# VectorE adds the token biases of more quads: half quads in block 1, four late quads of block 0

## What is computed

```
h   = tanh(ctx@Ws [:, None, t, :] + norm(x)@W [:, f, None, :] + b)     # (2, 2048, 77, 512)
rho = einsum('bftd,d->bft', h, w) + mask                               # scores
att = softmax(rho, over the 77 tokens)
x   = x + tanh(att@ctx@Wcw + bcw) * norm(x) + tanh(att@ctx@Wcb + bcb)
g   = silu(fp4(norm(x)) @ fp4(w_gate).T) * (fp4(norm(x)) @ fp4(w_up).T)
out = x + fp4(g) @ fp4(w_down).T
```

## Time and profile before

| | |
|---|---|
| median of 3 runs | 1538.8 us (1537.33 to 1539.91) |
| profiled execution | 1539.24 us, span 1537.4 us |
| busy: PE, ACT, DVE, POOL | 93%, 88%, 75%, 16% of the span |
| mean granted PE clock | 0.989 of full |
| block 0 scored | until about 352 us |
| quads 7 to 76 of block 1 scored | 385 to 671 us |
| tanhs: plain, 128 x 1024 | 1156 ns mean, 4 to a quad |
| tanhs: summed, 128 x 4096 | 3640 ns mean |
| sum on VectorE, 128 x 1024 | 750 ns mean, 4 to a quad |

### The profile page before, as it was taken

The page is one execution under the profiler, slowest core; times in us unless marked ns, Lnnn a source line. Parts: engine busy times, 40 slices in busy tenths (PEclk is TensorE's granted clock), DMA queues, the critical chain, the costliest instruction groups (busy, mean ns, idle before and its releaser), DMA issues.

```text
span 1537.4 us, 24122 instructions
## 1 busy us (share of the span) xinstructions
PE 1432.1 (93%) x9752; PEld 647.7 (42%) x9752; DVE 1157.2 (75%) x1783; ACT 1359.6 (88%) x1249; POOL 248.7 (16%) x389
## 2 busy tenths in 40 slices
PE   7988889856999999999999999989999999999998
PEld 4444444411333333334444444434444444555564
DVE  4699997944586666759666776698877787898887
ACT  5999989999999999999999999999999999433321
POOL 0122222200111010111011111011101111312211
PEclk9999999988999999999999999999999999999999
DMA  5133332320011111201111111112111111123332
GB/s 159 42 83 83 83 82 75 95 65 8 8 26 41 40 27 41 40 15 40 41 40 40 41 33 37 36 40 40 40 41 41 40 41 40 40 59 73 80 69 62
DMA packets 181557, 77.91 MB, mean 51 GB/s; under 512 B 163627, under 2 KB 165675, under 8 KB 181445
## 3 DMA queue, kind: packets, MB, share of 16 engines
q1 hardware_dynamic: 180224, 75.00, 21.0%
q10 hardware_dynamic: 1221, 1.36, 0.3%
HBM read 27.85 MB, written 8.39 MB: 24 GB/s over the span
## 4 chain that ended last, share of the span: by engine, by line
PE 52%; ACT 27%; DVE 17%; issue 2%; DMA 1%; POOL 1%; SPq 0%; ACTq 0%; DVEq 0%; POOLq 0%
PE rho L809 19%; ACT hring L628 17%; PE dn L906 10%; PE gu1g L892 5%; PE gu0g L892 5%; PE gu1u L892 5%; PE gu0u L892 5%; ACT hring L623 4%; DVE featT L985 2%; ACT wd_room L628 2%; DVE work L1019 2%; ACT featT L623 1%; ACT featT L628 1%; DVE work L1040 1%; DVE work L1039 1%
## 5 line engine op out<-in xcount | busy, mean ns | idle before, releaser
L628 ACT ACTIVATE hring<-featT,bias 128x1024 f32<-128x1024 f32 x688 | 729.2, 1156 | 2.6 <-PE rho L809 2.5
L809 PE MATMUL rho<-hring,wslide 128*32 128x512 f32 x3776 | 459.0, 611 | 61.5 <-ACT hring L628 52.4
L809 PEld LDWEIGHTS rho<-hring,wslide 128*32 128x32 f32 x3776 | 105.5, 111 | 338.6 <-issue 191.7
L628 ACT ACTIVATE featT<-featT,bias 128x1024 f32<-128x1024 f32 x220 | 236.3, 1178 | 2.2 <-PE rho L809 2.2
L906 PE MATMUL dn<-wd_room,turned 128*128 128x512 f16 x1023 | 230.6, 380 | 0.2 <-DMA turned<-work 0.2
L490 POOL TENSOR_SCALAR split_t<-sm 128x32 f32<-128x32 f32 (+4 forms) x82 | 19.7, 240 | 1178.1 <-DVE sm L1008 1178.1
L623 ACT ACTIVATE hring<-featT 128x4096 f32<-128x4096 f32 x57 | 207.5, 3640 | 0.4 <-DVE featT L985 0.4
L985 DVE TENSOR_SCALAR featT<-featT,bias 128x1024 f32<-128x1024 f32 x256 | 175.5, 750 | 11.9 <-ACT hring L623 7.6
L1309 DVE TENSOR_TENSOR work<-sg,gu1u 128x352 f32<-128x352 f32 x64 | 33.3, 521 | 173.9 <-ACT sg L661 173.1
L906 PEld LDWEIGHTS dn<-wd_room,turned 128*128 128x128 f16 x1023 | 96.4, 98 | 145.2 <-issue 36.0
L809 PE MATMUL rho<-featT,wslide 128*32 128x512 f32 x1056 | 126.4, 596 | 5.4 <-ACT featT L628 3.1
(11 more groups left out here) (228 smaller groups left out, 1578.5 us busy)
## 6 DMA issues: line engine op xcount, KB each, us to landing
xt<-in_x SPq DMA_DIRECT2D x32, 256.0 KB, 2.8
out<-xt SPq DMA_DIRECT2D x32, 256.0 KB, 2.3
work<-in_x SPq DMA_DIRECT2D x8, 512.0 KB, 4.1
xt<-in_x SPq DMA_DIRECT2D x6, 512.0 KB, 4.3
xt<-in_L_ffn_w_gate SPq DMA_DIRECT2D x11, 256.0 KB, 2.7
xt<-in_L_ffn_w_up SPq DMA_DIRECT2D x11, 256.0 KB, 3.0
work<-in_L_ffn_w_down SPq DMA_DIRECT2D x2, 704.0 KB, 5.1
xt<-in_L_ffn_w_down SPq DMA_DIRECT2D x2, 704.0 KB, 4.1
```

Source lines behind the costliest of these rows:

```text
L628: act.activation(slot[s][:, g, :], featT[:, e, ROW0[k]:ROW0[k] + rows], ACT.Tanh, bias=bias[:, e, base + tok:base + tok + 1]).then_inc(tan ...
L809: last = pe.matmul(rho[SLOTW * g:SLOTW * g + SLOTW, hf * 512:hf * 512 + 512], wslide[:, e, SLOTW - 1 - r:2 * SLOTW - 1 - r], slot[s][:, g, ...
```

## The change

Three sets of sums are added; nothing else is computed differently.

1. `LATE_SUMS`: the last four quads of block 0 (73 to 76). Quads 73 and 75 go to a room made of two pieces, `stage` and the first 2048 columns of `turned`; ACT takes two tanhs over 2048 columns. Quads 74 and 76 go to `work`, one tanh each. The sum of 73 stands behind the last `down_weights`, the other three behind the wait for `wd_turned`, all ahead of `softmax_drain(0)`.
2. Whole quads 6 and 8 of block 1, and with them the half quads 7 and 9: a new call of `sum_quads` behind `rows_tile(0)` makes these four.
3. Half quads 7, 9, 13, 16, 19, ... 73 of block 1 (23 of them): VectorE adds the biases of the first two parts into `stage` (two instructions), ACT takes one tanh over 2048 columns and two biased ones. The room `stage` is single, so a half waits until ACT has read the half before. Each half stands in VectorE's list where `sum_quads` comes to its number: 13 behind `rows_tile(1)`, 16 behind sum 15, 19 behind product 1 of tile 1 (ahead of `rows_tile(2)`), 22 behind product 2, 25 in the middle of `quantise_hidden(1)`, and so on.

The counts of `summed` are now kept in parts of a quad, because a half adds two. The lists of blocks 2 and 3 keep their quads and rooms.

```
+    LATE_SUMS = (73, 74, 75, 76)
...
+    ROOM_STAGE, ROOM_TURNED, ROOM_WORK = 4, 5, 6
...
+    for m, room in zip(LATE_SUMS, (ROOM_TURNED, ROOM_WORK, ROOM_TURNED, ROOM_WORK)):
+        give_room(m, room)
+    WHOLE = {1: [6, 8, *range(12, QPB, 3)], 2: [3, *range(11, QPB, 4)], 3: [2, 5, *range(11, QPB, 3)]}
+    HALF = {1: [7, 9, *range(13, QPB - 3, 3)], 2: [], 3: []}
     for k in range(1, NBLK):
...
+        for q in sorted([*WHOLE[k], *HALF[k]]):
+            if q in HALF[k]:
+                give_room(QPB * k + q, ROOM_STAGE)
+            else:
+                give_room(QPB * k + q, 0 if k == 1 else 1 + WHOLE[k].index(q) % (k - 1))
...
+        pieces = [[featT[:, :, ROW0[i]:ROW0[i] + 1024]] for i in range(NBLK - 1)] + [[slot[3]]]
+        pieces += [[rows_of(stage[:, :])], [rows_of(stage[:, :]), rows_of(turned[:, 0:2048])], [rows_of(work[:, 0:4096])]]
...
                 if n in SUMMED:
-                    act.wait_ge(summed, GRP * (SUMMED[n] + 1))
-                    act.activation(slot[s], rooms[room_of[n]], ACT.Tanh).then_inc(tanh_ready, GRP)
-                    return
+                    act.wait_ge(summed, SUMMED[n])
+                    at = 0
+                    for piece in pieces[room_of[n]]:
+                        count = piece.shape[1]
+                        act.activation(slot[s][:, at:at + count, :], piece, ACT.Tanh).then_inc(tanh_ready, count)
+                        at += count
+                    part = range(at, GRP)
...
-                for g in range(GRP):
+                rows = [piece[:, i, :] for piece in pieces[room_of[n]] for i in range(piece.shape[1])]
+                for g, row in enumerate(rows):
...
             down_weights(3)
+            sum_quad()
             dve.wait_ge(wd_turned, 16 * KC)
+            for _ in LATE_SUMS[1:]:
+                sum_quad()
...
             rows_tile(0)
+            sum_quads(before[0, 0] - 2)
```

More of the change, by code:

```diff
@@ L111, in bass_xattn_fp4_ffn, with give_room @@
     assert n == QUADS
[L112 to L116, removed]
-    for k in range(1, NBLK):
[L118 to L123, removed]
+    ROOM_STAGE, ROOM_TURNED, ROOM_WORK = 4, 5, 6
+    last_in = {r: QPB * (r + 1) - 1 for r in range(NBLK - 1)}
+    last_in.update({NBLK - 1: None, ROOM_STAGE: None, ROOM_TURNED: None, ROOM_WORK: None})
+    summed_quads, room_of, room_from = [], {}, {}
+    def give_room(m, room):
+        room_of[m], room_from[m] = room, last_in[room]
+        last_in[room] = m
+        summed_quads.append(m)
+    for m in FIRST_SUMS:
+        give_room(m, NBLK - 1)
+    for m, room in zip(LATE_SUMS, (ROOM_TURNED, ROOM_WORK, ROOM_TURNED, ROOM_WORK)):
+        give_room(m, room)
+    WHOLE = {1: [6, 8, *range(12, QPB, 3)], 2: [3, *range(11, QPB, 4)], 3: [2, 5, *range(11, QPB, 3)]}
+    HALF = {1: [7, 9, *range(13, QPB - 3, 3)], 2: [], 3: []}
+    for k in range(1, NBLK):
+        for q in sorted([*WHOLE[k], *HALF[k]]):
[3 more added lines that the diff above has]
+                give_room(QPB * k + q, 0 if k == 1 else 1 + WHOLE[k].index(q) % (k - 1))
     LAST = NBLK - 1
     FREE_FROM = BASE[LAST] - 2
-    SUMMED = {m: i for i, m in enumerate(summed_quads)}
+    rows_summed = [2 if room_of[m] == ROOM_STAGE else GRP for m in summed_quads]
+    SUMMED = {m: sum(rows_summed[:i + 1]) for i, m in enumerate(summed_quads)}
     SOFTMAX_AT = {BASE[k] - 2: k for k in range(1, NBLK)}
@@ L215, in bass_xattn_fp4_ffn, with rows_of @@
                 wd_room[:, 0:4096].rearrange("p (g c) -> p g c", g=GRP), featT[:, :, ROW0[-1]:]]
-        rooms = [featT[:, :, ROW0[i]:ROW0[i] + 1024] for i in range(NBLK - 1)] + [slot[3]]
+        def rows_of(area):
+            return area.rearrange("p (g c) -> p g c", c=1024)
+        pieces = [[featT[:, :, ROW0[i]:ROW0[i] + 1024]] for i in range(NBLK - 1)] + [[slot[3]]]
+        pieces += [[rows_of(stage[:, :])], [rows_of(stage[:, :]), rows_of(turned[:, 0:2048])], [rows_of(work[:, 0:4096])]]
         xnT2 = [stage[:, i * 1024:i * 1024 + 1024].rearrange("p (k r) -> p k r", k=KC) for i in range(2)]
@@ L981, in sum_quad @@
                     dve.wait_ge(tanh_ready, GRP * (room_from[n] + 1))
-                for g in range(GRP):
+                rows = [piece[:, i, :] for piece in pieces[room_of[n]] for i in range(piece.shape[1])]
+                for g, row in enumerate(rows):
                     r, e = quad_at(q) if q < QPB - 1 else (FULLR, g)
                     tok = BATCH_OF[k] * TOK + GRP * r + (g if q < QPB - 1 else 0)
-                    dve.tensor_scalar(rooms[room_of[n]][:, g, :], featT[:, e, ROW0[k]:ROW0[k] + BLOCKS[k]],
+                    dve.tensor_scalar(row, featT[:, e, ROW0[k]:ROW0[k] + BLOCKS[k]],
                                       bias[:, e, tok:tok + 1], None, ALU.add).then_inc(summed, 1)
```

## The result

The changed kernel took 1541.8 us in the median of 14 runs (1540.28 to 1543.44), the kernel before 1538.91 us in runs on the same chips. The ratio is 1.002, its 95% interval [1.0012, 1.0029]: some 3 us slower, where the forecast was 0.7 us slower and the range 1533.5 to 1542.5. The execution profiled took 1542.41 us with a span of 1540.6, that is 3.2 us more span than before.

The account below looks back on a forecast made before the run. ACT bounds block 1 as long as VectorE delivers its sums in time. +1.0 us after two tiles and -0.3 for the rest make +0.7 on 1538.8: 1539.5 us, range 1533.5 to 1542.5.

Parts of the forecast that it names:

- the last score: End of block 1: its last score was to come within 2 us of 670.9.
- Unit prices: On ACT a whole sum saves 0.65 us, a half quad 0.22; on VectorE a half sum costs 1.35 us.
- the straight line: Half tanh on ACT: 1.86 us, between 1.04 for 1024 columns (biased) and 3.51 for 4096 (unbiased).
- Part 1: Last four quads of block 0: all sums in time, block 0 ends 2.2 us earlier.
- Part 2: Quads 6 to 9 of block 1: ACT waits 2.4 us at quad 6, against 1.3 + 0.44 us saved.
- (d): Rival, end of block 0: slow PE clock makes the late sums worth 1.7 us less, 1541; with (c) beyond the forecast 0.07.
- Part 3: Tiles 0 and 1 of block 1: halves 16 and 19 add 2.7 us on VectorE; quad 21 at 442.0, 1.0 us later.
- Part 4: Block 1 from quad 22: 18 halves save 4.0 us, waits cost 4.35, old waits of 0.7 go: net -0.3 us.
- 0.5 us for PE: Block 1 from quad 22: ACT's waits for PE, counted within the 4.35 us of waits.
- The sum: End of block 1: +1.0 - 0.3 = +0.7 us on 1538.8, giving 1539.5.
- (a): Rival, block 1: VectorE hides the sums and all 8.5 us arrive, 1530.3; partly hidden 1533 to 1535; chance 0.22.
- (b): Rival, tiles 2 to 6: VectorE falls behind in each, 2.6 + 1.3 us against 0.8 saved, 1555; chance 0.08.
- (c): Rival, block 1: a half saves 0 (1543) or 0.33 us (1538); with (d) beyond the forecast 0.07.

Follow-up runs that it names:

- more early sums: Changed kernel without whole 6 and halves 16, 19, 49, 61, but with quad 9 summed whole and quad 10 half: 1533.9 us, 0.997 of the kernel before.
- the price alone: Changed kernel, but VectorE adds the 23 halves and ACT makes those quads with four biased tanhs: 1542.16 us, 1.002 of the kernel before.
- the spared version: Changed kernel without whole quad 6 and the halves of 16, 19, 49 and 61: 1533.55 us, 0.9965 of the kernel before.

## Why the prediction was right, and which term was mis-sized

The mechanism was right: VectorE was nowhere near full, and still gave the savings back by coming late at six places, and ACT's wait at each has the length forecast to within 0.15 us. At the mark the change costs 2.3 us where 0.7 were forecast, inside the range. That it was no more is in part luck: ACT's waits, less those of before, came to 12.4 us against the 9.3 forecast (4.6 + 1.0 + 4.35 - 0.7), and the savings were 1.6 us larger too. One of its signs failed: the last score was to end within 2 us of 670.9 and ended at 673.49. By its steps:

**Unit prices.** A half tanh takes 1.80 us start to start, not 1.86, so a half quad saves 0.28 and not 0.22. The estimate from the Trainium skill (ScalarE: Activation LUTs, What ACT_TABLE_LOAD costs), 1.80 because the unbiased tanh has no bias pointer to pay for, was the better price; the straight line mixed two kinds of tanh. The end that the prediction drew from it, 1538.7, is the further off, since the missing waits weigh more. All savings together: 2.4 + 1.3 + 23 x 0.28 = 10.1 us, 1.6 more than forecast.

**Part 1.** Right; block 1's first tanh came 2.3 us earlier (2.2 forecast), and the late quads alone are 0.9991.

**Part 2.** Right in the wait of 2.4 us, incomplete in what follows it. PE idles for 4.05 us while ACT waits, and its score of quad 6 is then slow:

```profile
379.80 3.42 PE L829 MATMUL rho<-hring,wslide 128*32 128x512 f32 x16 [4.05 <-ACT hring L642]
```

3.42 us instead of 1.92. The granted clock of PE over 376 to 384 us was 0.79 of full here and 1.00 in the kernel before (first this kernel, then the one before):

```profile
376.00:384.00 8.00, 4.20 (x22) 1.19 (x23) 4.42 (x8) 7.87 (x5) 0.00 (x0) 0.79 0.01 2
```

```profile
376.00:384.00 8.00, 5.68 (x45) 2.12 (x46) 0.00 (x0) 8.00 (x9) 0.00 (x0) 1.00 0.16 30
```

Those 1.5 us come back to ACT as the wait of 1.16 us at quad 10: ACT may be only two quads ahead of PE, and PE, late with quad 6 and without a gap from there on, scores quad 8 behind two gate groups. The kernel before had its slow stretch too, one that cost it nothing: over 370 to 376 us its granted clock was 0.54 and its score at 371.93, of quad 4, took 3.64 us. In all five kernels in which ACT waits at quad 6 PE is idle for 4.04 to 4.08 us there and scores it in 3.39 to 3.64 us. Of the seven without that wait five score it in 1.92 or 1.93 us. The other two, the one with more early sums (2.87 us after 2.24 of idle time) and the one without the sums of quads 6 to 9, have a slow score too:

```profile
377.08 3.01 PE L829 MATMUL rho<-hring,wslide 128*32 128x512 f32 x16 [2.23 <-ACT hring L648]
380.02 2.53 PE L912 MATMUL gu0g<-wgu,turned 128*128 128x352 f16 x12
```

There ACT, with longer quads behind it, waits only 0.19 us at quad 10. So the slow clock costs something where ACT is at the end of its two slots. The prediction had the clock as a rival, (d), but at the end of block 0; it struck at quad 6 and again ahead of quad 65.

**Part 3.** The path on VectorE was right: 29.4 + 2.7 us. Its start was 1.1 us later than forecast, 0.8 by the wait at quad 10 (less what was saved beyond the forecast) and 0.25 because this execution was that much later already at 308 us, and so was its end: quad 21 at 443.03 and not 442.0. On VectorE:

```profile
430.70 0.52 DVE L1333 TENSOR_TENSOR work<-sg,gu0u 128x352 f32<-128x352 f32 x1
431.25 0.52 DVE L1333 TENSOR_TENSOR work<-sg,gu1u 128x352 f32<-128x352 f32 x1
431.81 1.42 DVE L1006 TENSOR_SCALAR stage<-featT,bias 128x1024 f32<-128x1024 f32 x2
...
440.18 2.74 DVE L1006 TENSOR_SCALAR featT<-featT,bias 128x1024 f32<-128x1024 f32 x4
```

From 431.25 on the order is product, half sum of 19, rows, sum of 21, and ACT waits at both sums. Too low was the price of that product: it was to come at 429.6 and came at 430.70, and PE's wait for it grew from 0.8 to 2.4 us. ACT did not feel it, since it waited for the half of quad 19 meanwhile; in the kernel with the price alone, which takes no half, it did.

**Part 4.** The waits at 49, 61 and 72 were right. Mis-sized is "0.5 us for PE": in this part ACT waits for PE 0.37 + 0.54 + 1.15 = 2.1 us. The 1.15 stand behind the late half of quad 61 and the slow stretch of PE that followed it, and are gone where either is missing. The prediction paid for each late sum once, at PE's full speed. What it left out, here and at quad 10, is that PE, left idle by a late sum, can come back slow: 1.16 + 1.15 us and 0.1 for each, 2.5 of the 3.1 us by which the waits were too low. After the waits at quads 19, 49 and 72 nothing of the kind came in this execution.

**The sum.** The terms as they should have stood: waits for VectorE 9.6 us in six places, for PE 3.2 in four, and 0.1 for each of the ten, since tanhs in a row start 0.1 us ahead of the end that the profile shows of the one before (1.90 long, 1.80 apart) and one that waits does not; less the 1.1 + 0.3 us of before in three places; less 10.1 saved: 13.8 - 1.4 - 10.1 = +2.3 us, as the mark moved. Of the other 0.9 us of the profiled execution's 3.2, 0.25 lie ahead of 308 us and 0.7 after block 1, where PE ran slow once (2.69 us for a score, and 2.84 for the gate group behind it):

```profile
709.53 2.69 PE L829 MATMUL rho<-hring,wslide 128*32 128x512 f32 x16 [1.98 <-ACT hring L648]
```

One execution each does not tell whether that belongs to the change.

**The rivals.** (a) is right in that ACT's savings are worth something (7.2 us when VectorE's part is left out) and wrong in that VectorE hides them; the argument against it, that the idle time lies in other places, is what the spared version shows. (b) did not happen: tiles 2 to 6 had 0 to 1.8 us of waiting for VectorE each and not 3.9. (c) was off by 0.06 us a half, to the good side. What stays open is what makes PE slow. It had been idle for 2.12 and 4.05 us ahead of the two slow scores of the changed kernel that cost ACT time, and after 4 us it was slow in five kernels out of five; but after 2.12 us ahead of quad 62's score it was slow in the changed kernel and not in the one without the sums of quads 6 to 9, and after 2.4 ahead of the gate group of tile 1 it was slow without quad 6's sum and not in the changed kernel.

## What to carry to other kernels

When work is moved from the bound engine to one with idle time, its price is not its duration but how much later the next thing on that engine's list becomes that somebody waits for. Walk that engine's list from one wait to the next beside the bound engine's, and add work only where the first is shorter: here five of 29 added sums turned a gain of 0.35% into a loss of 0.2%. Look then at who else is left idle by the wait. Here a late sum held ACT, ACT held PE, and PE's next matmuls were sometimes slower; with a ring of two slots that came back to ACT as a second wait of 1.15 us four quads later. Where PE was not slow, none came.

## What the runs showed of the hardware

A tanh over 128 x 2048 without bias takes 1.90 us, 1.80 start to start, the same over 4096 columns 3.61 and 3.51. A tanh that had to wait does not have that overlap of 0.1 us with the one before. PE's granted clock over 376 to 384 us was 0.79 of full, between its levels of 2.4 and 1.2 GHz, after PE had been idle for 4.05 us, and a quad's score took 3.42 us in place of 1.92; over 610 to 620 us it was 0.83 after 2.12 us of idle time. The same 2.12 us in another kernel left it at 1.00.
